# Loading order at the start of a Perceiver layer, and three small edits beside it: two halves of the key weights and the query weights on the scalar engine's queue

## The reference

```python
x = x + xattn(ctx_1024, layernorm(x), mask, ...)      # keys from 2*1024 context rows and 128 latent rows
# inside xattn:
xn = layernorm(x, ln_x_g, ln_x_b)                      # x is the context here
ln = layernorm(latents, ln_l_g, ln_l_b)
q  = (ln @ Wq)                                         # 128 x 256 by 256 x 1024
kv = concatenate([xn @ Wkv, ln @ Wkv], axis=1)
kn = rmsnorm(k, kn_g);  qn = rmsnorm(q, qn_g) * d ** -0.5
out = softmax(qn @ kn.T) @ v
```

## Time and profile before

| | before |
|---|---|
| median of 3 runs | 232.57 us (232.32 to 232.83) |
| the profiled execution: its time, its span | 233.34 us, 231.4 us |
| PE busy, of the span | 220.6 us (95%) |
| DVE, ACT, POOL busy | 152.0, 154.9, 80.2 us |
| read from memory | 13.15 MB |

### The profile page before, as it was taken

One profiled execution on the slowest core, in us unless ns is written; L12 is line 12 of the kernel. 1 busy time (PEld: TensorE's weight loads), 2 busy tenths in 40 slices (PEclk: granted clock), 3 DMA queues, 4 the chain that ended last, 5 costly groups with the idle time before them and its releaser, 6 DMA issues.

```text
span 231.4 us, 4188 instructions
## 1 busy us (share of the span) xinstructions
PE 220.6 (95%) x1446; PEld 190.8 (82%) x1446; DVE 152.0 (66%) x347; ACT 154.9 (67%) x340; POOL 80.2 (35%) x131
## 2 busy tenths in 40 slices
PE   7899999999989999999999999999999998999884
PEld 6556778887778888989888989899999987899773
DVE  2699899998778786776866755566766661303431
ACT  2868777979885968776676567778787755314151
POOL 5188897861592837445160500000000010000300
PEclk9999999999999999999999999999999999999999
DMA  6590134200000000000000899700000000000000
GB/s 184 151 317 32 47 122 175 68 25 0 23 0 3 1 4 0 0 3 0 0 0 3 256 428 328 177 3 0 0 4 0 1 3 0 0 3 0 0 3 23
DMA packets 11252, 13.80 MB, mean 60 GB/s; under 512 B 1592, under 2 KB 9952, under 8 KB 10976
## 3 DMA queue, kind: packets, MB, share of 16 engines
q1 hardware_dynamic: 10680, 11.97, 16.6%
q10 hardware_dynamic: 552, 1.58, 1.9%
HBM read 13.15 MB, written 0.13 MB: 57 GB/s over the span
## 4 chain that ended last, share of the span: by engine, by line
PE 65%; DVE 21%; ACT 5%; issue 4%; DMA 2%; POOL 2%; ACTq 0%; POOLq 0%; DVEq 0%
PE banks L1307 19%; PE banks L1157 14%; PE banks L1216 8%; PE banks L1248 8%; PE banks L1447 5%; DVE small L902 4%; DVE sk L914 4%; PE banks L1321 3%; DMA wraw<-in_L_xattn_Wkv 2%; PE banks L1250 2%; ACT knT L632 2%; PE banks L1370 2%; PE banks L1474 2%; DVE small L871 1%; DVE raw L865 1%
## 5 line engine op out<-in xcount | busy, mean ns | idle before, releaser
L937 DVE TENSOR_TENSOR ptl<-banks,pth 128x512 fp32r<-128x512 f32 (+1 forms) x48 | 26.8, 558 | 24.2 <-ACT pth L668 23.2
L1307 PE MATMUL banks<-xnh,pth 128*128 128x256 f32 x128 | 37.6, 294 | 0.1
L1307 PE MATMUL banks<-xnh,ptl 128*128 128x256 f32 x128 | 36.2, 283 | 0.0
L1307 PE MATMUL banks<-xnl,pth 128*128 128x256 f32 x128 | 36.2, 283 | 0.0
L515 POOL TENSOR_TENSOR small<-small 128x16 f32<-128x16 f32 x7 | 20.4, 2915 | 32.1 <-DVE small L909 32.1
L668 ACT ACTIVATE pth<-banks 128x512 fp32r<-128x512 f32 (+1 forms) x48 | 23.7, 495 | 10.6 <-PE banks L1157 9.5
L615 ACT ACTIVATE sk<-banks 128x512 f32<-128x512 f32 x36 | 20.7, 602 | 12.1 <-PE banks L1216 11.6
L902 DVE TENSOR_REDUCE small<-sk 128x8 f32<-128x512 f32 x36 | 23.6, 678 | 5.9 <-ACT sk L615 5.9
L914 DVE TENSOR_TENSOR sk<-banks,small 128x512 f32<-128x512 f32 x36 | 23.0, 680 | 6.6 <-POOL small L515 6.5
L495 POOL COPY sp<-sp 128x64 f32<-128x64 f32 x16 | 3.8, 238 | 62.8 <-ACT sp L649 62.7
L1157 PE MATMUL banks<-ident,sp 128*128 128x128 f32 x144 | 24.2, 279 | 1.1 <-ACT sp L649 1.1
(11 more groups left out here) (193 smaller groups left out, 478.0 us busy)
## 6 DMA issues: line engine op xcount, KB each, us to landing
knT<-in_L_attn_qkv_kernel SPq DMA_DIRECT2D x1, 3072.0 KB, 12.4
raw<-in_ctx SPq DMA_DIRECT2D x16, 128.0 KB, 2.3
knT<-in_L_xattn_Wq SPq DMA_DIRECT2D x1, 1024.0 KB, 6.8
wv<-in_L_xattn_Wkv ACTq DMA_DIRECT2D x1, 1024.0 KB, 4.9
wout_sb<-in_L_xattn_Wout SPq DMA_DIRECT2D x1, 1024.0 KB, 5.8
knT<-in_L_attn_out_kernel SPq DMA_DIRECT2D x1, 1024.0 KB, 15.2
wraw<-in_L_xattn_Wkv ACTq DMA_DIRECT2D x1, 512.0 KB, 5.0
wraw<-in_L_xattn_Wkv SPq DMA_DIRECT2D x1, 512.0 KB, 5.3
```

The costliest lines, as they stand in the source:

```text
L937: nc.vector.tensor_tensor(ptl[:, j0:j1, :], banks[:, t3_bank(u, c), 0:(j1 - j0) * P].rearrange("p (j r) -> p j r", j=j1 - j0), pth[:, j0:j ...
L1307: nc.tensor.matmul(banks[:, u_bank(u), 0:D], p_[:, j, :], x_, start=(j == 0 and i == 0), stop=False)
```

## The change

It does six things. (a) ACT issues three weight loads one behind the other: first half of the key weights, second half, `Wq`. SP issues all four gain loads into `gb8`, then context tiles 0 and 1, and its wait ahead of the gain rows is for the first half instead of the second. (b) ACT makes the root for the latents with an activation, and DVE takes the reciprocal. (c) The first high half `wkh` is made by two engines, one block of 128 rows of the weights by ACT, the other by DVE; DVE takes the statistics of context tile 0 ahead of its first `wk_low`. (d) PE runs 7 instead of 9 filler matmuls ahead of the gain columns. (e) The latent rows `lnf` are made by transposing `lnTf` back on PE, ahead of the transpose of tile 4, and an ACT copy; POOL's two operations and the loads of the rows `gl` and `bl` are gone. (f) POOL makes the root of tile 5 at the end of its round 2 instead of in the middle of its round 3.

```diff
         @block.sync
-            for i, v in enumerate((ln_l_g, ln_l_b)):
+            for i, v in enumerate((ln_l_g, ln_l_b, ln_x_g, ln_x_b)):
                 sp.dma_start(*gain_rows(i, v)).then_inc(w_cols, 16)
...
-                if k == 0:
-                    sp.dma_start(wraw[:, :, 512:1024], wkv_v[:, :, 512:1024]).then_inc(w_k[1], 16)
                 if k == 1:
-                    sp.wait_ge(w_k[1], 16)
+
+                    sp.wait_ge(w_k[0], 16)
                     sp.dma_start(rows[:, 0, :], row(ln_x_g)).then_inc(w_rows, 16)
                     sp.dma_start(rows[:, 1, :], row(ln_x_b)).then_inc(w_rows, 16)
-                if k == 2:
-                    sp.dma_start(wq_sb, wq_v).then_inc(w_q, 16)
                 if k == 3:
-                    sp.dma_start(gl, row(ln_l_g)).then_inc(w_lrows, 16)
-                    sp.dma_start(bl, row(ln_l_b)).then_inc(w_lrows, 16)
         @block.gpsimd
-            pool.wait_ge(lat_mv, 1)
-            rsqrt_var(lmv, lve, lrs, 1e-10, 1.0 + 1e-5).then_inc(lat_rs, 1)
...
-                if 2 < i and i + 2 < B * NT:
+                if 3 < i and i + 2 < B * NT:
                     tile_rstd(i + 2)
                 if i + 1 < B * NT:
                     norm_shift(i + 1)
-                if i == 4:
-                    pool.wait_ge(lat_hat, 1)
-                    pool.wait_ge(w_lrows, 32)
-                    link(nc.gpsimd.tensor_tensor(lmul, latg, gl, ALU.mult))
-                    nc.gpsimd.tensor_tensor(lnf, lmul, bl, ALU.add).then_inc(ln_ready, 1)
+                if i == 2:
+                    tile_rstd(i + 3)
         @block.scalar
             act.dma_start(wraw[:, :, 0:512], wkv_v[:, :, 0:512]).then_inc(w_k[0], 16)
-            for i, v in enumerate((ln_x_g, ln_x_b)):
-                act.dma_start(*gain_rows(2 + i, v)).then_inc(w_cols, 16)
+            act.dma_start(wraw[:, :, 512:1024], wkv_v[:, :, 512:1024]).then_inc(w_k[1], 16)
+            act.dma_start(wq_sb, wq_v).then_inc(w_q, 16)
...
-            wk_high(0)
+            act.wait_ge(eps_ready, 1)
+            act.wait_ge(lat_mv, 1)
+            nc.scalar.activation(lve, lmv[:, 1:2], ACT.Sqrt, bias=lat_eps, scale=1.0 + 1e-5).then_inc(lat_sd, 1)
+
+            act.wait_ge(w_k[0], 16)
+            nc.scalar.activation(wkh[:, 0, 0:512], wraw[:, 0, 0:512], ACT.Copy).then_inc(wk_hi, 1)
             act.wait_ge(cols_ps, 1)
...
+                if tile(i + 2) == LT:
+                    act.wait_ge(xt_ps, LT + 1)
+                    nc.scalar.activation(lnf, banks[:, t1_bank(LT), D:2 * D], ACT.Copy).then_inc(ln_ready, 1)
         @block.vector
-            dve.wait_ge(lat_rs, 1)
+            dve.wait_ge(lat_sd, 1)
+            link(nc.vector.reciprocal(lrs, lve))
             center(latg, xb[:, :], lmv[:, 0:1], lrs).then_inc(lat_hat, 1)
+            dve.wait_ge(w_k[0], 16)
+            nc.vector.tensor_copy(wkh[:, 1, 0:512], wraw[:, 1, 0:512]).then_inc(wk_hi_dve, 1)
+            tile_stats(0)
...
             wk_low(0)
-            tile_stats(0)
             xt_low(0)
         @block.tensor
+                if n == LT:
+
+                    pe.wait_ge(lnT_ready, 1)
+                    transposes(banks[:, t1_bank(n), D:2 * D], lambda c: lnTf[:, c, :], DC)
                 transposes(banks[:, t1_bank(n), :], lambda c: src[:, c * P:(c + 1) * P], DC).then_inc(xt_ps, 1)
...
-            keep_clock(9, 3)
+            keep_clock(7, 3)
             pe.wait_ge(w_cols, 64)
```

More of the change, by code:

```diff
@@ L33, in perceiver_layer @@
     QI = 2
+    LT = 4
     ITEMS_A = FA + 2
@@ L112, in perceiver_layer @@
         lnf = early(3, D, D)
-        gl = early(4, 0, D)
         gb8 = early(2, 0, P)[0:8, :]
-        lmul = early(2, D, D)
         x0Tf = early(2, 2 * D, D).rearrange("p (c r) -> p c r", c=DC)
-        bl = early(4, D, D)
         latg = early(4, 2 * D, D)
@@ L156, in perceiver_layer @@
         mcol = small[:, 202:203]
+        lat_eps = small[:, 203:204]
         gcols = small[:, 204:212]
@@ L197, in perceiver_layer @@
         ones_ready = sem("ones_ready")
-        w_lrows = sem("w_lrows")
+        lat_sd = sem("lat_sd")
         w_cols = sem("w_cols")
@@ L209, in perceiver_layer @@
         lat_mv = sem("lat_mv")
-        lat_rs = sem("lat_rs")
+        eps_ready = sem("eps_ready")
         lat_hat = sem("lat_hat")
@@ L217, in perceiver_layer @@
         wk_hi = sem("wk_hi")
+        wk_hi_dve = sem("wk_hi_dve")
         wk_lo = sem("wk_lo")
@@ L500, in _ @@
                                     pattern=[[-1, P]], channel_multiplier=1).then_inc(consts, 1)
+            nc.gpsimd.memset(lat_eps, 1e-10).then_inc(eps_ready, 1)
             nc.gpsimd.memset(mcol, -BIG)
             nc.gpsimd.memset(qbd[:, :, :], 0.0).then_inc(zeroed, 1)
-            pool.wait_ge(lat_mv, 1)
-            rsqrt_var(lmv, lve, lrs, 1e-10, 1.0 + 1e-5).then_inc(lat_rs, 1)
             tile_rstd(0)
@@ L959, in _ @@
             dve.wait_ge(lat_mv, 1)
-            dve.wait_ge(lat_rs, 1)
+            dve.wait_ge(lat_sd, 1)
+            link(nc.vector.reciprocal(lrs, lve))
             center(latg, xb[:, :], lmv[:, 0:1], lrs).then_inc(lat_hat, 1)
+            dve.wait_ge(w_k[0], 16)
+            nc.vector.tensor_copy(wkh[:, 1, 0:512], wraw[:, 1, 0:512]).then_inc(wk_hi_dve, 1)
+            tile_stats(0)
             def wk_low(h):
                 dve.wait_ge(wk_hi, h + 1)
+                if h == 0:
+                    dve.wait_ge(wk_hi_dve, 1)
                 cols = slice(h * 512, (h + 1) * 512)
@@ L1203, in project @@
                     pe.wait_ge(wk_hi, h + 1)
+                    pe.wait_ge(wk_hi_dve, 1)
                 order = ((xth, wkh), (xth, wkl), (xtl, wkh))
```

## The result

The changed kernel takes 236.25 us (median of 4 runs, 235.99 to 236.92), the kernel before 232.53 us beside it (232.32 to 232.83): a ratio of 1.0162, 95% interval 1.0141 to 1.0182, or 3.7 us slower. The direction was forecast, the size not: 234.3 us was the prediction and 235.7 its upper end.

A forecast was written before the change was run, and what follows sets the result against it. PE, busy 95% of the span, was taken to bound the kernel, so delays before 47 us reach the end. Start +2.2, clock +0.3 and rounds -0.8 gave +1.7 us: 234.3 us on the median, whole range 230.6 to 235.7.

The forecast's parts named there:

- `w_cols` at 8.6: Start: the gain columns PE waits for arrive behind `Wq` at 8.6 us, against 5.83 before; bounds 4.5 and 8.6.
- A load that has begun is carried to its end, and the other queue waits: Loads of the start: the two queues take turns load by load, so a gain load follows each weight load.
- Context tiles 0 and 1 end there at 8.7 and 9.0: Start: both context tiles, 0.13 MB each, share the gain loads' engines and land at 8.7 and 9.0 us.
- DVE subtracts to 13.5, and PE takes the last term at 13.5: First tile: with late columns, the last term comes at 13.5 instead of 11.32 us, a loss of +2.2 us.
- the mark: Start: when PE takes the last term of the first tile, 11.32 us before; later rounds shift by what it shifts.
- PE's clock: Start: after idling from 4.97 to 8.6, PE may run at half speed again; +0.3 us, bounds nothing and about 1.3.
- The median taken as the profiled execution less 0.77: Conversion to the median: forecast 235.0 us for the profiled execution, 0.77 lower for the median, 234.3 us.
- Rounds 3 to 5: -0.8: Later rounds, edits (e) and (f): without DVE's wait for POOL they save 0.8 us; bounds 0 and -1.2.
- (b), (c), (d): 0: Start: the root, rounding and filler edits gain 0 in the late case, hidden behind the columns.
- the early case: Rival at the start: columns come early, before about 6.8 us; mark 1.0 earlier, rounds -0.8, time 230.8; chance 0.24.
- the late case: Start: gain columns come behind `Wq` at 8.6 us, PE idles from 4.97; chance 0.58.
- the likeliest case: Columns behind `Wq`, chance 0.58: start +1.6 to +2.8, clock 0 to +1.3, rounds -1.2 to 0; 233.0 to 236.0 us.

The follow-up runs named there:

- e3: The changed kernel with the load of `Wq` issued by SP after the gain rows, as before the change; 233.2 us, ratio to before 1.0027.
- e2: The changed kernel with DVE's statistics of context tile 0 behind the first subtraction of the weights again; 234.23 us.
- e9: The changed kernel with 10 instead of 7 fillers ahead of the gain columns and 6 more between first high and first low term; 234.89 us.
- e5: The kernel of e3 with 10 instead of 7 filler matmuls ahead of the gain columns; 232.14 us.
- e12: The kernel before, unchanged, profiled a second time; 232.49 us, span 230.7 us.
- e4: The kernel before with edits (e) and (f) alone; 231.31 us, ratio 0.9946.
- e8: The changed kernel with part (a) undone, all loads of the start as before; 231.25 us, ratio 0.9928.
- e10: The kernel of e7 with 9 instead of 7 filler matmuls, five executions; 231.6 us, ratio 0.9964.
- e6: The kernel before with the load of `Wq` alone moved to ACT's queue, behind its two gain loads; 236.19 us.
- e7: The kernel of e3 with gain loads ln_x_g and ln_x_b on ACT's queue again, between the key-weight halves; 232.59 us, in two groups.

## Why the prediction was wrong

Step by step, as the prediction took them:

- *"`w_cols` at 8.6."* This is the first step that failed, and the path hung on it. The columns came at 6.45, and at 6.43 without `Wq` (e3). "A load that has begun is carried to its end, and the other queue waits" does not hold for small loads: SP's queue moves 8 packets in the microsecond of q10's 183. The page "DMA: Bandwidth & Descriptors" of the Trainium skill, section "Queues, rings and completion order", has each DMA engine take turns between the queues, a whole packet of descriptors at a time. These rows agree with it as far as small loads get through beside large ones; where a turn begins or ends they do not show, and the reading that by it the columns come behind `Wq` went too far.
- *"Context tiles 0 and 1 end there at 8.7 and 9.0."* Right for tile 0: 9.03. But the sum let this hide behind the columns. In fact it was the wait that ended last: 3.23 us on DVE, with the first subtraction behind it (e2: 2.0 us; e3: 3.05 us).
- *"DVE subtracts to 13.5, and PE takes the last term at 13.5."* The first half came out, by another road: the second subtraction ended at 13.13, 1.87 us later than before (10.04 + 1.22 = 11.26 in the earlier trace rows), against the +2.2 forecast. That is luck, and with it the direction: from columns at 6.45 the prediction's own path of 4.9 us (8.6 to 13.5) ends at 11.35, where the mark was before (11.32), and with the rounds at -0.8 the kernel would have been faster; its own limit for that was columns before 6.8. In e3, with columns at 6.43 and tile 0 early, the second subtraction does end at 11.13. PE did not follow at once either.
- *"PE's clock: +0.3, nearer to nothing, since the path there runs over ACT and DVE."* This is the second step that failed, a term of the right kind and too small. From 13.13 to 14.71 PE is late by its own rate, 1.58 us, and 0.25 more in tile 1 (round 3 starts 3.64 late, the mark 3.39). Filling ahead of PE's waits returns 1.4 (e9), and 1.06 in e5. The upper bound of 1.3 was nearer, and its own words (12 matmuls of about 0.3, doubled, half of it hidden) give 1.8, not 1.3; and there were two pauses, not one: PE also waited 1.33 us for the first subtraction, which the sum did not have.
- *The median taken as the profiled execution less 0.77.* This is the third step that failed. Those 0.8 us were one late load, the very one at the head of the earlier trace rows, and the changed kernel does not pay it: its own path starts elsewhere. Against the execution of e12 the mark moves from 10.59 to 14.71, +4.12, not +3.39.
- *"Rounds 3 to 5: -0.8."* Right in kind, small in size: -1.3 with (e) and (f) alone (e4), past the bound of -1.2, and 1.1 between the rounds of the profiles. DVE's wait of 0.91 us for POOL is gone. That the long instances of the centering go with POOL's line 549 was wrong: two of 0.90 and 0.81 us remain, beside POOL's other work:

```profile
29.77 0.90 DVE L864 TENSOR_SCALAR raw<-raw,small 128x256 f32<-128x256 f32 x1
...
34.20 0.81 DVE L864 TENSOR_SCALAR raw<-raw,small 128x256 f32<-128x256 f32 x1 [0.17 <-POOL small L456]
```

- *"(b), (c), (d): 0."* Right only where the loads are early: e8 and e4 differ by 0.06 us, although e8's mark (10.35) lies 0.24 before e12's. The 1.0 us that the early case was to give was not there, for its base was the late execution. In the late case, which came, the order of DVE in part (c) is not 0: it puts the late tile ahead of the first subtraction, and undoing it returns 2.0 us (e2).
- *The ranges.* The terms of the likeliest case (+2.8, +1.3 and 0 at their upper ends) add up to 236.7, not 236.0, and the whole range stopped below both, at 235.7. The measured 236.25 lies inside what the terms allow.

With measured terms, against e12's profile: from its mark at 10.59 to the second subtraction's end at 13.13 it is +2.54, PE's rate adds 1.58 + 0.25, the rounds give back 1.1; +3.3, against +3.4 in the spans (234.1 and 230.7). The medians differ by 3.7. Of the 0.3 between, 0.26 is that the profiled execution of the changed kernel, 235.99, was the shortest of its four; what lies outside the span is 1.9 us there and 1.8 in e12. By experiments, taking part (a) out of the changed kernel is worth 5.0: 3.05 for `Wq` on the scalar engine's queue, 1.06 for PE's pause ahead of the late columns (e3 to e5), and 0.9 for the rest (e5 to e8), of which 0.5 goes with the gain loads' queue (e5 to e10); that last split is near what a run can tell.

## What to carry to other kernels

Before a large load is moved to the front of another queue, list every load of the first queue that is still in flight then, and take the latest time at which an in-order engine stands in front of one: the wait that counts may be on a tile that is not needed yet, behind which something urgent is queued. Price a new pause of PE by the rate of the matmuls behind it, not by the pause alone. And take two profiles of the kernel before: where the profiled execution lies off the median, look for the place of the difference; here it was one load, and the change took that load off the path.

## What the runs showed of the hardware that was not expected

- PE ran pairs of matmuls at 0.85 us between starts (1.2 GHz) for 8 us while the granted clock was given as 1.00; the windows of the changed kernel's profile, 8 to 12 and 12 to 16 us (stretch, length, then busy us and instructions of PE, PEld, DVE, ACT, POOL, granted clock, DMA share, GB/s):

```profile
8.00:12.00 4.00, 2.56 (x6) 1.46 (x6) 2.49 (x6) 1.88 (x4) 1.86 (x3) 1.00 0.92 299
12.00:16.00 4.00, 3.95 (x12) 2.55 (x10) 2.24 (x4) 1.46 (x4) 1.96 (x5) 1.00 0.00 0
```

  In e9 (9 to 12 us) and e6 (12 to 18 us) pairs of 0.95 to 1.22 us stand beside a granted clock of 0.50. So in these profiles the rate has to be read from the durations of one form of matmul, not from that column alone.
- POOL's first operation of the root (line 455, 128 values) took 1.08 us at 9.76 in the changed kernel, beside DVE's subtraction (9.59 to 10.80), and 0.19 at 13.77:

```profile
9.76 1.08 POOL L455 TENSOR_SCALAR small<-small 128x1 f32<-128x1 f32 x1 [6.31 <-DVE small L877]
...
11.58 0.41 DVE L864 TENSOR_SCALAR raw<-raw,small 128x256 f32<-128x256 f32 x1 [0.45 <-POOL small L456]
...
13.77 0.19 POOL L455 TENSOR_SCALAR small<-small 128x1 f32<-128x1 f32 x1 [2.07 <-DVE small L877]
```

  It took 1.08 us beside that subtraction in e3, e5, e7, e9 and e10 too. DVE then waits 0.45 us for the root before it centers context tile 0 and goes on to its second subtraction.
